# Layer-norm row work of an attention stage moved to other slots and engines: ScalarE in two passes with an fp32 intermediate, GpSimd for the low part, SyncE for loads and stores

## The chip, the cores and the metric

The kernel runs on one core of one Trainium2 chip. The metric is the device time of one execution in microseconds (us). The core's engines are PE (TensorE), DVE (VectorE), ACT (ScalarE), POOL (GpSimd) and SP (SyncE, which here issues DMAs and computes nothing). Each runs its own list of instructions in order; they meet through semaphores.

## The reference, cut to what matters

```python
def reference(x, txt, ...):
    h = _L0_tok_ref(log_dt, Lambda, x, 1024)            # a kernel of 1024 positions from 64 modes, 32 x 128 rows
    h = jnp.concatenate([h, txt], axis=1)                # 32 batches of 128 + 77 = 205 rows of 1024
    h = h + _L0_attn_ref(_layernorm(h), wq, wk, wv, wo)  # causal, 32 query heads of 32, 8 key heads
    h = h + _L0_ffn_ref(_layernorm(h), W_base, b_base, enc0, enc1, coefs0, coefs1, mask0, mask1)
    return h

def _layernorm(x, axis=-1, eps=1e-05):
    m = jnp.mean(x, axis=axis, keepdims=True)
    v = jnp.var(x, axis=axis, keepdims=True)
    return (x - m) / jnp.sqrt(v + eps)
```

Everything is fp32 in and out. The kernel multiplies in fp16 pairs: a value is split into a high part (rounded to fp16) and a low part (what is left, also fp16), and a product is three products, high*high, high*low and low*high.

## The kernel before

Three stages run one after the other, with a barrier between them. `ssm` (about the first 185 us) computes the first 128 rows of each batch and writes them to `hcat` in DRAM. `attention` (about 185 to 1740 us) works through the 32 batches and writes to `acat`. `tail` (the rest) does the output projection and the second residual block over 52 tiles of 128 rows. The change touches `attention` and a little of `ssm`.

`attention` is a software pipeline written out by hand. Step b (from -4 to 32) works on several batches at once, each with its part of the work, and `parts(b)` says which parts a step has:

- `att`: scores, exponentials and weighted values of batch b;
- `max`: score rows and their maxima of batch b+1 (a max per row is folded into the score product as two further rows of `qst`);
- `qkv`: query, key and value units of batch b+2 (8 query units, 2 key, 2 value; a unit is 24 matmuls of 205 columns into one of two PSUM banks `psJ`);
- `turn`: DMA transposes of the normalized rows of batch b+3, from `xfh`, `xfl` (high, low) to `xth`, `xtl`;
- `ln`: layer-norm statistics and the split of batch b+4;
- `load`: rows of batch b+5 from `hcat` into `xin` (two buffers).

A step has eight slots, g = 0 to 7, one per key head. In slot g every engine does its share for that head. PE (`step`, L1059 to L1106): two score products (`scores`, L981), maxima products (L1024 to L1031), first half of the slot's query unit, the third score product (L984), more maxima products, second half of the unit, the weighted values of the head before (`weigh`, L1010), then any second or third unit of the slot. ACT: three exponentials into `p32` (L783), three fp16 copies of the masked result into `ph` (L790), then an fp16 copy of each unit (L798). POOL: three causal masks (L699) and the low parts of the second and third block, `pl` (L704). DVE: the maxima (`take_maxes`, L879 and L885), the low part of the first block (L936), `norm` of the head before (L833, L836), and the low part of each unit (`split_unit`, L893), which waits for ACT's copy. The last unit of a slot is split late, in the next slot behind the first maxima. `EXTRA` puts the four value and key units into slots 0 to 3, as a second unit; the transposed maxima (unit kind "m") lie in slots 0 and 4.

The row work of layer norm in the kernel before:

- statistics on DVE in slots 1 to 3 (`layer_norm`, L841), the last of them the first guess of a reciprocal square root;
- `scale_rows` on POOL behind slot 3 (L669): twelve chained operations on 128x2 (`rsqrt_rounds`) and the negated mean;
- `high_part` on ACT (L723), one of four pieces (two row tiles by two halves of 512 columns) in each of slots 4 to 7: subtract the mean in place (L732), then multiply by the scale into fp16 `xfh` (L734);
- `low_part` on DVE (L858): multiply by the scale and subtract `xfh`, into `xfl` (L862). Piece 0 in slot 6, pieces 1 and 2 in slot 7, piece 3 in slot 0 of the next step;
- `turn` on SP (L632) near the start of the next step: four DMA transposes.

SP's list in a step, in order (L583 to L626): keys and queries of the second half restacked (L578), max rows of half 1 (L629, L630), at one step the loads of the tail's weights (`ahead`, L604), `turn` of both row tiles, keys and queries of the first half restacked, four transposes of the values (L622), max rows of half 0. ACT issues the loads of `xin` (L714, L715) in slot 3 and the stores of `ao` (L720, L721) in slots 2 and 6, and copies the values to `vh`, `vl` (`values`, L742) at the head of slot 2.

Before the first step ACT makes the high parts of the query weights (`weights_high(0)`), DVE their low parts (`weights_low(0)`), and the first rows are loaded, normalized, split and turned. In `ssm`, `weight_peak` (L370) takes the largest weight in the last 12 of 16 chunks, and SP sends the two peaks through DRAM (L174, L176) before the last chunk's stores.

## Time and profile before

| | |
|---|---|
| median of 3 runs | 2897.89 us (2894.68 to 2900.92) |
| the profiled execution | 2894.3 us, of which the span of instructions is 2891.9 us |
| mean granted clock of PE | 0.975 |
| busy over the span | PE 92%, PE weight load 66%, DVE 67%, ACT 43%, POOL 40% |

```profile
## 2 busy tenths in 40 slices
PE   1948999999999999999999976999999999999999
DVE  8966888888888888888888674644444444444443
ACT  4343676766767676766667572201000010101010
POOL 2751565656656565666656570101010101010100
PEclk9979999999999999999999976999999999999999
DMA  7756556465555555565555454454545455545553
```

A digit is the busy share of a slice of 72.3 us in tenths; PEclk is the granted clock in tenths. Slices 5 to 22 are the attention stage in its steady state. PE is over 90% busy there, DVE 80 to 90%. A matmul's duration in this profile is longer than its pitch (252 ns against 88 ns for 205 columns), so a wait of PE shows shorter than the time it costs; time lost is best read from start to start.

### The profile page before, as it was taken

To read this page: it belongs to the slowest core of one execution; us is meant where nothing else is said; L and a number is where in the kernel's file an instruction comes from. 1 tells how busy PE (TensorE), PEld (TensorE's weight loads), DVE (VectorE), ACT (ScalarE), POOL (GpSimd) and SP (SyncE) were. 2 spreads that over 40 slices of the span, in tenths; PEclk is the share of its full clock that TensorE was granted. 3 is DMA by queue.
4 is the path that set the end of the run, shared out by engine and by line. 5 is a ranking of instruction groups with operands and counts; after the bars stand their busy time and mean duration, and the time that the engine had idled before them with its cause. 6 is when DMAs were issued, how large, how long until landed. Compare 5 with 4: busy or idle time off the path is not lost. (4 is left out here: it accounts for less than half of the span.)

```text
span 2891.9 us, 70053 instructions
## 1 busy us (share of the span) xinstructions
PE 2655.3 (92%) x27456; PEld 1919.6 (66%) x27456; DVE 1941.2 (67%) x5569; ACT 1230.0 (43%) x2570; POOL 1144.9 (40%) x1810
## 2 busy tenths in 40 slices
PE   1948999999999999999999976999999999999999
PEld 1838888888888888888888952444444444444444
DVE  8966888888888888888888674644444444444443
ACT  4343676766767676766667572201000010101010
POOL 2751565656656565666656570101010101010100
PEclk9979999999999999999999976999999999999999
DMA  7756556465555555565555454454545455545553
GB/s 242 194 122 100 98 92 105 85 109 93 96 94 96 103 93 104 84 107 92 101 92 86 73 124 170 113 139 116 133 122 136 119 134 121 133 123 131 125 129 77
DMA packets 509031, 332.99 MB, mean 115 GB/s; under 512 B 421145, under 2 KB 464409, under 8 KB 508225
## 3 DMA queue, kind: packets, MB, share of 16 engines
q1 hardware_dynamic: 486192, 264.68, 46.3%
q10 hardware_dynamic: 22512, 63.84, 7.1%
q8 instruction: 219, 3.59, 0.6%
q14 instruction: 108, 0.88, 0.1%
HBM read 116.49 MB, written 80.61 MB: 68 GB/s over the span
## 5 line engine op out<-in xcount | busy, mean ns | idle before, releaser
L1044 PE MATMUL psJ<-xth,qh 128*128 128x205 f16 x2048 | 517.3, 253 | 51.6 <-DMA xtl<-xfl 47.6
L704 POOL TENSOR_TENSOR pl<-arena,ph 128x410 f16<-128x410 f32 (+1 forms) x512 | 501.0, 998 | 94.7 <-ACT ph L790 94.7
L1046 PE MATMUL psJ<-xth,ql 128*128 128x205 f16 x2048 | 516.3, 252 | 0.0
L1045 PE MATMUL psJ<-xtl,qh 128*128 128x205 f16 x2048 | 515.8, 252 | 0.0
L699 POOL TENSOR_SCALAR_AFFINE_SELECT arena<-arena 128x256 f32<-128x256 f32 (+1 forms) x768 | 331.7, 438 | 438.3 <-ACT arena L783 419.3
L1261 POOL TENSOR_TENSOR arena<-stage,arena 128x1024 f32<-128x1024 f32 x52 | 122.1, 2349 | 936.2 <-DVE stage L1304 936.2
L1275 ACT CAST xh<-arena 128x1024 f16<-128x1024 f32 x52 | 54.3, 1045 | 995.1 <-DVE arena L1313 995.1
L783 ACT ACTIVATE arena<-psT,escale 128x410 f32<-128x410 f32 (+1 forms) x768 | 399.6, 565 | 95.5 <-PE psT L984 57.5
L790 ACT CAST ph<-arena 128x410 f16<-128x410 f32 (+1 forms) x768 | 334.8, 500 | 14.9 <-POOL arena L699 14.7
L1304 DVE SCALAR_TENSOR_TENSOR stage<-ps5O,osc,h_in 128x512 f32<-128x512 f32 x104 | 77.9, 750 | 388.4 <-PE ps5O L1401 388.4
L885 DVE TENSOR_REDUCE mx<-psS 77x2 f32<-77x410 f32 x512 | 296.5, 579 | 60.7 <-PE psS L1031 57.0
L1399 PE MATMUL ps5F<-wfh,xth 128*128 128x512 f16 x832 | 315.4, 379 | 3.4 <-DMA xtl<-xl 2.3
L1400 PE MATMUL ps5O<-wol,ath 128*128 128x512 f16 x832 | 316.1, 380 | 0.0
L1399 PE MATMUL ps5O<-woh,ath 128*128 128x512 f16 x832 | 316.1, 380 | 0.0
L1401 PE MATMUL ps5O<-woh,atl 128*128 128x512 f16 x832 | 316.0, 380 | 0.0
L1400 PE MATMUL ps5F<-wfl,xth 128*128 128x512 f16 x832 | 315.3, 379 | 0.0
L1401 PE MATMUL ps5F<-wfh,xtl 128*128 128x512 f16 x832 | 315.3, 379 | 0.0
L879 DVE CUSTOM_DVE_ANT_0 seen<-psS,mask 128x128 bf16<-128x128 f32 x1024 | 235.4, 286 | 82.7 <-PE psS L1024 82.0
L1010 PE MATMUL psO<-vh,ph 128*128 128x33 f16 (+1 forms) x3072 | 261.0, 178 | 5.0 <-issue 4.6
L1010 PE MATMUL psO<-vl,ph 128*128 128x33 f16 (+1 forms) x3072 | 260.0, 178 | 0.0
L1010 PE MATMUL psO<-vh,pl 128*128 128x33 f16 (+1 forms) x3072 | 260.0, 178 | 0.0
L1046 PE MATMUL psJ<-xth,kl 128*128 128x205 f16 x1024 | 257.8, 252 | 0.0
(231 smaller groups left out, 6106.2 us busy)
## 6 DMA issues: line engine op xcount, KB each, us to landing
a_in<-acat SPq DMA_DIRECT2D x52, 512.0 KB, 3.8
h_in<-hcat SPq DMA_DIRECT2D x52, 512.0 KB, 4.6
qst<-qsh SPq DMA_DIRECT2D x128, 205.0 KB, 4.7
out<-stage SPq DMA_DIRECT2D x51, 512.0 KB, 3.1
hcat<-ob SPq DMA_DIRECT2D x64, 256.0 KB, 4.4
xin<-hcat ACTq DMA_DIRECT2D x32, 512.0 KB
acat<-arena ACTq DMA_DIRECT2D x64, 256.0 KB
qst<-qsl SPq DMA_DIRECT2D x64, 205.0 KB, 5.7
```

What stands on the lines that cost most here:

```text
L699: pool.affine_select(out=v, in_=v, compare_op=ALU.is_ge, fill=0.0, base=0, pattern=[[0, v.shape[1]], [1, w]], channel_multiplier=-1).then_ ...
L704: pool.tensor_tensor(view(pl, g % 2, k), view(p32, g % 2, k), view(ph, g % 2, k), ALU.subtract).then_inc(lo_pool, 1)
L783: act.activation(view(p32, g % 2, k), ps_view(psT[(g + k) % 2], k), ACT.Exp, scale=(escale[:, 0:1] if k < 2 else escale[0:TXT, 0:1])).then ...
L790: act.copy(view(ph, g % 2, k), view(p32, g % 2, k)).then_inc(hi_done, 1)
L885: dve.tensor_reduce(dst, v, AX.X, ALU.max).then_inc(s_read, 1)
L1010: m = pe.matmul(o[:, t, r, :], p, v[0:T[j], j, g, :], start=n == 0, stop=n == len(list_) - 1)
L1044: pe.matmul(ps[:, 0:S], wh[:, k, c], xth[:, par, k, 0:S], start=k == 0, stop=False)
L1045: pe.matmul(ps[:, 0:S], wh[:, k, c], xtl[:, par, k, 0:S], start=False, stop=False)
L1046: m = pe.matmul(ps[:, 0:S], wl[:, k, c], xth[:, par, k, 0:S], start=False, stop=k == KC - 1)
L1399: pe.matmul(ps[h][:], th[:, k, :], wh[:, k, c], start=k == 0, stop=False)
L1400: pe.matmul(ps[h][:], th[:, k, :], wl[:, k, c], start=False, stop=False)
L1401: m = pe.matmul(ps[h][:], tl[:, k, :], wh[:, k, c], start=False, stop=k == KC - 1)
```

## The change

- `high_part` now does both in fp32 first: one activation with scale and bias writes the normalized value in place, fp32, then a plain copy rounds it to `xfh`. For that `nmean` becomes minus mean times scale (one more small POOL operation per step), and `rs` and `nmean` get two buffers.
- The low part becomes a plain subtraction, `xin - xfh`. POOL does it (`low_rows`), except for the first batch, where DVE does (`low_part`).
- The row work is moved by a step: the pieces of `high_part` of batch b+3 run in slots 1, 2 and 3 (two pieces) of step b, behind the query unit's copy and ahead of the copy of the slot's second unit; the pieces of `low_rows` run at the ends of POOL's slots 2, 3 and 4 (two pieces), and `scale_rows` behind them in slot 4.
- The value and key units move from slots 0 to 3 into slots 1 to 4. In slots with several units DVE splits the query unit early, behind the low part of the first block.
- `values` is cut in two and moved behind the `ph` copies of slots 1 and 2.
- SP issues the loads of `xin` and the stores of `ao` instead of ACT. `turn` of the first row tile stays near the step's start, but each of its transposes waits for its own part; `turn` of the second tile goes behind the value transposes. The tail's loads go out one per step from step 1 on, and the largest (4 MB, output weights) at the end of step 29 instead of early in step 30.
- Start: DVE itself does the twelve chained operations for the first batch; half of the query weights' low parts are put behind the first row pieces; the first load is issued alone, the second when it has landed. In `ssm` the peaks are taken two chunks earlier and sent one chunk earlier.

```diff
-        EXTRA = {0: ("v", 0), 1: ("v", 1), 2: ("k", 0), 3: ("k", 1)}
+        EXTRA = {1: ("v", 0), 2: ("v", 1), 3: ("k", 0), 4: ("k", 1)}
+        HIGH, LOW, LINK = {1: (0,), 2: (1,), 3: (2, 3)}, {2: (0,), 3: (1,), 4: (2, 3)}, {1: 0, 2: 1, 3: 2}
+        FIRST_HIGH, FIRST_LOW = {2: (0,), 3: (1,), 4: (2, 3)}, {3: (0,), 4: (1,), 5: (2, 3)}
...
 # SP, step(b, par, has)
-                if b == B - 2:
-                    for q in v_in:
-                        sp.wait_ge(q, 32 * B)
-                    for dst, src, arrived in ahead:
-                        sp.dma_start(dst, src).then_inc(arrived, 16)
-                if has["turn"]:
+                if has["last"]:
+                    store(b - 1, 1)
+                if has["turn"] and b >= 0:
                     wait(sp, pj_filled, base)
                     turn(0, nxt, b + 3)
-                    turn(1, nxt, b + 3)
                 if has["qkv"]:
 ...                 # keys, queries of the first half restacked, as before
+                if has["turn"] and b < 0:
+                    wait(sp, pj_filled, base)
+                    turn(0, nxt, b + 3)
+                    turn(1, nxt, b + 3)
 ...                 # value transposes, as before
+                if has["turn"] and b >= 0:
+                    turn(1, nxt, b + 3)
                 if has["max"]:
                     wait(sp, pj_lo, base + at(rows, "m", 0) + 1)
                     shift_rows(0, nxt)
+                if has["att"]:
+                    store(b, 0)
+                if has["load"]:
+                    sp.wait_ge(x_lo, 4 * (b + 4))
+                    load(b + 5, 1 - par)
+                if 1 <= b < len(ahead):
+                    dst, src, arrived = ahead[b]
+                    sp.dma_start(dst, src).then_inc(arrived, 16)
...
             def turn(t, to, n):
+                sp.wait_ge(x_hi, 4 * n + 2 * t + 2)
+                sp.dma_start_transpose(out=xth[:, to, :, cols], in_=xfh[0:r, t, :]).then_inc(xt_in[t], 16)
                 sp.wait_ge(x_lo, 4 * n + 2 * t + 2)
-                sp.dma_start_transpose(out=xth[:, to, :, cols], in_=xfh[0:r, t, :]).then_inc(xt_in[t], 16)
                 sp.dma_start_transpose(out=xtl[:, to, :, cols], in_=xfl[0:r, t, :]).then_inc(xt_in[t], 16)
+            load(0, 0)
+            sp.wait_ge(x_in[0], 32)
+            load(1, 1)
...
 # POOL
+            def low_rows(m, n):
+                t, h = divmod(n, 2)
+                c, r = slice(h * D // 2, (h + 1) * D // 2), T[t]
+                pool.wait_ge(x_hi, 4 * m + n + 1)
+                pool.tensor_tensor(xfl[0:r, t, c], xin[0:r, m % 2, t, c], xfh[0:r, t, c], ALU.subtract).then_inc(x_lo, 1)
...
-                    if g == 3 and has["ln"]:
+                    if has["turn"]:
+                        for piece in LOW.get(g, ()):
+                            low_rows(b + 3, piece)
+                    if g == 4 and has["ln"]:
                         scale_rows(b)
...
 # ACT
-                act.activation(x, x, ACT.Identity, bias=nmean[0:r, t:t + 1]).then_inc(centred, 1)
-                act.wait_ge(centred, 4 * (b + 4) + n + 1)
-                act.activation(xfh[0:r, t, c], x, ACT.Copy, scale=rs[0:r, 3, t:t + 1]).then_inc(x_hi, 1)
+                act.activation(x, x, ACT.Identity, bias=nmean[0:r, m % 2, t:t + 1],
+                               scale=rs[0:r, m % 2, 3, t:t + 1]).then_inc(centred, 1)
+                act.wait_ge(centred, 4 * m + n + 1)
+                act.copy(xfh[0:r, t, c], x).then_inc(x_hi, 1)
...
-                    if g >= 4 and has["ln"]:
-                        high_part(b, par, g - 4)
+                        if i == 0:
+                            for piece in pieces:
+                                high_part(b + 3, piece)
...
 # DVE
+                    if b == -4:
+                        rsqrt_rounds(link, dve, rs[:, b % 2])
...
-                    if has["turn"] and g == 0:
-                        low_part(b + 3, 3)
+                    split = 0
+                    if len(rows[g]) > 1 and rows[g][0][0] == "q":
+                        split_unit(b, par, (k0 + n) % 2, *rows[g][0], base + n + 1)
+                        n += 1
+                        split = 1
-                        for piece in {6: (0,), 7: (1, 2)}.get(g, ()):
-                            low_part(b + 4, piece)
```

## Rows read from the trace of the kernel before

**Rows 1.** Waits of PE, 400 to 1600 us: total, times, longest
```profile
PE psS L1028 <- DVE mx L879: 37.0, 52, 1.1
PE psT L984 <- ACT arena L783: 28.9, 55, 1.1
```

**Rows 2.** PE in time through step 10: start, duration, line, shapes, [idle before]
```profile
750.11 0.33 PE L981 MATMUL psT<-qst,kst 98*128 98x410 f16 x1
...
753.37 0.23 PE L1028 MATMUL psS<-mask,ident_bf 77*77 77x154 bf16 x1 [1.08 <-DVE mx L879]
...
757.93 0.34 PE L981 MATMUL psT<-qst,kst 98*128 98x410 f16 x1
...
764.29 0.34 PE L981 MATMUL psT<-qst,kst 98*128 98x410 f16 x1
...
771.57 0.34 PE L981 MATMUL psT<-qst,kst 98*128 98x410 f16 x1
...
777.94 0.34 PE L981 MATMUL psT<-qst,kst 98*128 98x410 f16 x1
...
779.82 0.30 PE L984 MATMUL psT<-qst,kst 98*77 98x308 f16 x1
...
782.35 0.34 PE L981 MATMUL psT<-qst,kst 98*128 98x410 f16 x1
...
796.52 0.33 PE L981 MATMUL psT<-qst,kst 98*128 98x410 f16 x1
```

**Rows 3.** DVE groups by line, 400 to 1600 us: busy, mean ns, idle before
```profile
L862 DVE SCALAR_TENSOR_TENSOR xfl<-xin,rs,xfh 128x512 f16<-128x512 f32 (+1 forms) x104 | 126.4, 1235 | 0.0
```

**Rows 4.** ACT in time, slots 3 and 4 of the step
```profile
774.22 1.30 ACT L790 CAST ph<-arena 128x410 f16<-128x410 f32 x3
775.42 0.32 ACT L798 CAST qsh<-psJ 128x205 f16<-128x205 f32 x1
778.14 0.33 ACT L798 CAST ksh<-psJ 128x205 f16<-128x205 f32 x1 [2.39 <-PE psJ L1046]
...
781.07 1.32 ACT L790 CAST ph<-arena 128x410 f16<-128x410 f32 x3 [0.40 <-POOL arena L699]
...
782.78 0.70 ACT L732 ACTIVATE xin<-xin,nmean 128x512 f32<-128x512 f32 x1
```

**Rows 5.** POOL in time, slots 3 and 4 of the step, then slot 7
```profile
775.25 1.73 POOL L704 TENSOR_TENSOR pl<-arena,ph 128x410 f16<-128x410 f32 x2 [0.38 <-ACT ph L790]
777.09 0.19 POOL L1135 TENSOR_TENSOR rs<-rs 128x2 f32<-128x2 f32 x1
...
780.40 0.22 POOL L673 TENSOR_SCALAR nmean<-mv 128x2 f32<-128x2 f32 x1
...
795.47 3.11 POOL L704 TENSOR_TENSOR pl<-arena,ph 128x410 f16<-128x410 f32 x2 [0.38 <-ACT ph L790]
```

**Rows 6.** SP's DMA issues in time, slots 4 and 5 of the step
```profile
779.90 6.78 SPq L622 DMA_TRANSPOSE vt<-stage  x4
786.73 0.59 SPq L629 DMA_DIRECT2D qst<-mh  x1
```

**Rows 7.** DMA issues of the execution: count, size, median us to landing
```profile
qst<-ml SPq DMA_DIRECT2D x64, 6.4 KB, 1.9
```

**Rows 8.** Tile xtl: issue of its transposes on SP, ns min/median/max
```profile
L636 SPq DMA_TRANSPOSE xtl<-xfl x64: 1281/1448/3170, 212.6 to 1604.7; - x64
```

**Rows 9.** The start of the attention stage in time: DVE, POOL, SP, PE
```profile
192.26 1.42 DVE L852 BATCH_NORM_STATS2 stats<-xin 128x6 f32<-128x512 f32 x2 [4.39 <-DMA xin<-hcat]
...
196.31 1.29 POOL L1135 TENSOR_TENSOR rs<-rs 128x2 f32<-128x2 f32 x1 [1.18 <-DVE rs L1128]
...
215.26 1.34 SPq L636 DMA_TRANSPOSE xtl<-xfl  x1
...
223.92 0.33 PE L1044 MATMUL psJ<-xth,qh 128*128 128x205 f16 x1 [47.64 <-DMA xtl<-xfl]
```

**Rows 10.** PE in time: the start of step 31
```profile
1712.06 0.52 PE L981 MATMUL psT<-qst,kst 98*128 98x410 f16 x1 [4.09 <-DMA qst<-ml]
```

More of the change, by code:

```diff
@@ L616, in step @@
                     restack(Q_PARTS, qst[par][:, 0], HALVES[0], q_in[0])
+                if has["turn"] and b < 0:
+                    wait(sp, pj_filled, base)
+                    turn(0, nxt, b + 3)
+                    turn(1, nxt, b + 3)
+                if has["qkv"]:
+                    wait(sp, pj_lo, base + at(rows, "v", 1) + 1)
                     wait(sp, v_ok, 2 * (b + 2))
@@ L626, in step, with load, store @@
                     shift_rows(0, nxt)
+                if has["att"]:
[6 more added lines that the diff above has]
+                    sp.dma_start(dst, src).then_inc(arrived, 16)
+                if b == B - 3:
+                    for q in v_in:
+                        sp.wait_ge(q, 32 * B)
+                    dst, src, arrived = ahead[0]
+                    sp.dma_start(dst, src).then_inc(arrived, 16)
+            def load(b, par):
+                sp.dma_start(xin[:, par, 0, :], hcat[b * S:b * S + P, :]).then_inc(x_in[par], 16)
+                sp.dma_start(xin[0:TXT, par, 1, :], hcat[b * S + P:b * S + S, :]).then_inc(x_in[par], 16)
+            def store(b, half):
+                c = slice(half * D // 2, (half + 1) * D // 2)
+                sp.wait_ge(norm_done, 8 * b + 4 * half + 4)
+                sp.dma_start(acat[b * S:b * S + P, c], ao[:, half, 0, :]).then_inc(a_out[half], 16)
+                sp.dma_start(acat[b * S + P:b * S + S, c], ao[0:TXT, half, 1, :]).then_inc(a_out[half], 16)
             def shift_rows(half, to):
@@ L678, in step @@
                 if not has["att"]:
-                    if has["ln"]:
+                    if has["ln"] and b > -4:
                         scale_rows(b)
+                    if has["turn"] and b > -3:
+                        for piece in range(4):
+                            low_rows(b + 3, piece)
                     if b == -4:
-                        pool.memset(ph[:], 0.0)
-                        pool.memset(pl[:], 0.0)
+                        pool.memset(ph[:, :, 2, :], 0.0)
+                        pool.memset(pl[:, :, 2, :], 0.0)
                     if b == -3:
@@ L759, in step @@
                 if b == -3:
+                    for n in range(4):
+                        high_part(0, n)
+                    n = 0
                     weights_high(1)
@@ L765, in step @@
                 for g in SLOTS:
-                    if g == 3 and has["load"]:
-                        act.wait_ge(x_lo, 4 * (b + 4))
-                        load(b + 5, 1 - par)
-                    if g == 2 and has["last"]:
-                        store(b - 1, 1)
-                    if g == 2 and has["max"]:
-                        values(b + 1)
-                    if g == 6 and has["att"]:
-                        store(b, 0)
                     if has["att"]:
@@ L790, in step @@
                             act.copy(view(ph, g % 2, k), view(p32, g % 2, k)).then_inc(hi_done, 1)
-                    for kind, m in rows[g]:
+                    if g in (1, 2) and has["max"]:
+                        values(b + 1, g - 1)
+                    pieces = (HIGH if b >= 0 else FIRST_HIGH).get(g, ()) if has["turn"] and b > -3 else ()
+                    if not rows[g]:
+                        for piece in pieces:
+                            high_part(b + 3, piece)
+                    for i, (kind, m) in enumerate(rows[g]):
                         src, hi, _ = unit_views(kind, m, (k0 + n) % 2, b, par)
@@ L799, in step @@
                         n += 1
-                    if g >= 4 and has["ln"]:
-                        high_part(b, par, g - 4)
+                        if i == 0:
+                            for piece in pieces:
+                                high_part(b + 3, piece)
             steps(act, step)
@@ L814, in _, with weights_low @@
             dve.wait_ge(cleared, 1)
-            def weights_low(n):
-                for k in range(KC):
+            def weights_low(n, ks):
+                for k in ks:
                     dve.wait_ge(w_hi, n * KC + k + 1)
@@ L939, in step @@
                         take_maxes(b, j, base, (0, 1), late_read)
[L940 to L950 removed]
+                    split = 0
[3 more added lines that the diff above has]
+                        split = 1
+                    if b == -3 and g == 0:
+                        for part, ks in (((0, 1), (4, 5)), ((2, 3), (6, 7))):
+                            for piece in part:
+                                low_part(0, piece)
+                            weights_low(0, ks)
+                        weights_low(1, range(KC))
+                    if has["ln"] and g in LINK:
+                        layer_norm(b, par, LINK[g])
+                    if b == -4 and g == NKV - 1:
+                        weights_low(0, range(4))
                     if has["att"] and g:
```

66 lines of the change are left out of this document (28 added, 38 removed).

## The prediction

> **What bounds the kernel now.** I read the busy digits first: in the attention stage PE is above 90% in every slice at the full clock, DVE nearly so, and the tail behind it is PE alone. The change leaves the tail as it is, so only three places can move: the steady steps of attention, the stage's start, and its last steps. Next the waits of PE in the steady stage [rows 1]: there are two kinds only, PE waiting for DVE's maxima (52 times in 26 steps, two per step) and for ACT's exponentials (55). Together they show 65.9 us of idle, 2.5 us per step. Then PE in time through one step [rows 2], since durations hide part of a wait. The step takes 796.52 - 750.11 = 46.41 us. Slots 1 and 3 have no gap: 6.36 and 6.37 us with a second unit. Slot 4, without one but with the transposed maxima (about 0.18), takes 4.41, so a plain slot costs 4.23 and a second unit 2.13. A clean slot 0 would be 4.23 + 2.13 + 0.18 = 6.54; it took 7.82: 1.28 lost, with PE waiting for maxima at 753.37. Slot 2 took 7.28 instead of 6.36: 0.92 lost, waiting for exponentials. Slots 5 to 7 took 14.17 instead of 12.69: 1.48 lost. In all 3.7 us of 46.4 are gaps, and 42.7 is the floor that PE's own work sets.
>
> **Part 1, what the moves remove.** DVE's low parts are 4 per step at 1.235 us [rows 3], 4.9 us. They stand in slots 6, 7 and 0, just where DVE is late with its maxima, so with them the gap of slot 0 and most of slot 7's go: I take 1.7 us. The gap of slot 2 comes from ACT issuing two stores and copying values ahead of its exponentials; both are moved away: 0.9. The gaps of slots 5 and 6 come from ACT's row pieces ahead of the next exponentials, two passes of 0.70 [rows 4], 1.4 us each. In slots 1 to 3 there is an idle stretch of 2.39 us per slot, in which ACT waits for the second unit [rows 4]. A piece and half of `values` (about as long as a `ph` copy, 1.30 / 3) fit in it with 0.5 to spare; two pieces (2.8, less what a plain copy saves against a scaled one, unknown) in slot 3 run 0.4 over, which the exponentials' lead over PE covers. Gain 0.8. I leave 0.2 for waits of DVE on the later unit copy (values and the early split stand between). So 3.7 becomes 0.2 if nothing new is late.
>
> **Part 2, what is late instead: POOL in slot 4.** The subtraction of 512 columns costs POOL 1.2 us: its two `pl` subtractions (410 and 308 columns) take 1.73 together [rows 5], 2.4 ns per column. Four pieces add 4.8 us per step to an engine that is busy 5 to 6 tenths of these slices: as a sum it fits. But where they lie counts. In slot 3 (start 771.57) POOL ends its `pl` at 776.98, 5.4 us behind the slot's start, and `scale_rows` runs from 777.09 to 780.62, 3.5 us [rows 5]. After the change slot 4 has 5.4, then two pieces (2.35), then `scale_rows` with one more operation (3.8): it ends 11.65 us after the slot's start. Slot 4, now with a second unit, lasts 6.54. The masks of slot 5 are wanted 1.15 us into it, at 7.7, so they are 4.0 us late. The kernel before shows what lateness does: there `scale_rows` makes the masks of slot 4 about 1.5 late, and ACT's `ph` copy comes at 781.07, 3.13 behind the slot's start of 777.94, where slot 3 has it at 774.22, 2.65 behind its start [rows 2, 4]. So 1.0 of the lateness is free, 0.5 is passed on, and PE does not yet stall. With 4.0 it is 3.0 that is passed on. Queued behind the waiting copies are, on ACT, the unit's copy (it ends some 4.05 into a slot on time, 775.42 + 0.2 [rows 4]) and the exponentials of slot 6, and on DVE the low part of the first block, `norm` and the maxima of slot 6. PE wants the first exponential of slot 6 at 1.88 into it (779.82 - 777.94 [rows 2]) and the first maxima right behind that. ACT: the unit's copy ends at 3.0 + 4.05 = 7.05, the exponential takes 0.6, 7.65 against 4.23 + 1.88 = 6.11: 1.55 late. DVE: its low part follows the first `ph` copy, at 3.0 + 3.2, and low part, `norm` and first maxima take some 2.0 (the sum of their means), 8.2 against 6.25: 1.95 late. I take a stall of 2.0 per step. Bounds: if a piece costs 1.0 and the chain 3.5, the stall is 1.3; beside DVE's low part the same two subtractions needed 3.11 [rows 5], 4.3 ns per column, and if that pace held for the pieces (2.2 each), it is 4.0.
>
> The Trainium skill speaks against this move: "GPSIMD Engine Reference", section 4.1 (Engine selection), gives elementwise work with two inputs to VectorE and calls GpSimd about 2 times slower. The rows here do not show that for these two operations, since DVE's piece has a mean of 1235 ns [rows 3] against my 1.2 us on POOL. By the rule a piece would take some 2.5 us, an estimate from the page's factor, and the time would be that of rival B's far end and some 10 more. Another rule speaks for it: "SBUF — State Buffer", section "Who interferes with whom", says that a DVE instruction with two SBUF inputs and a GpSimd instruction that reads SBUF exclude each other. By it the pair at 795.47 was held by DVE's low part, and relief comes with the move.
>
> **Part 3, SP's list.** It gets six more issues per step and two of four row transposes behind the values. Counted from slot 4's start: keys of the first half go at 2.5 (the key unit is one slot later), three issues of 0.6, queries follow to 6.4; the value transposes take 6.78 [rows 6] to 13.2; the second tile's two transposes about 3.4 (median 1.448, up to 3.170 [rows 8]) to 16.6; the max rows twice 0.6 to 17.8, landing 1.9 after the second's issue [rows 7], at 19.1. PE wants them at the head of the next step, 6.54 + 3 x 4.23 = 19.2 without a stall, 21.2 with the stall of part 2. Before, the first max row was issued at 786.73 [rows 6], 8.8 behind slot 4's start. So nothing is lost here, but the slack of some 10 us is gone. Loads and stores behind it have until the next step's slot 1 and later: cost nothing. `xt` of the second tile lands at about 18.5, also in time.
>
> **Sum, steady.** Per step 3.7 becomes 2.2: a gain of 1.5. Row work exists in steps 0 to 28, 29 steps: 43 us.
>
> **Part 4, the start.** PE waits 47.64 us, until 223.92 [rows 9]. The peaks' round trip held the last stores: 1.2 earlier. The statistics start at 192.26, after 4.39 of waiting for the first load, with both loads in flight [rows 9]; alone it lands perhaps 2 earlier (bounds 0 and 3). The twelve links on POOL took from 196.31 to 207.4, 11.1 us for what takes 3.5 in a steady step, beside DVE's weight parts [rows 9]; on DVE, at about 0.2 per link, 2.6. So ACT starts its pieces at about 195.7 and ends at 201. DVE then does 4 weight parts (4.8), pieces and the other four (6.8) until about 208; the last row transpose goes at about 206 instead of 215.26 and lands at 210. PE starts 14 earlier. Part is given back: in the steps below 0, SP puts four transposes (5.3) between the queries and the values, so the max rows of step -1 leave that much later and PE waits about 3.5 for them at step 0, and some 2 for the rows at step -1. I keep 9 (4 to 14).
>
> **Part 5, the end.** The 4.09 us at the head of step 31 is PE waiting for max rows that stood behind the tail's loads [rows 10]; these are elsewhere now. The 4 MB load at the end of step 29 puts the restacked keys behind it, wanted 17 us later: 1 us lost perhaps. Net 3 (-3 to 4).
>
> Total 43 + 9 + 3 = 55. Against the profiled execution's 2894.3 us that is 2839.3; the median of three is 3.6 above it, which I carry along: 2843.
>
> **Rivals.**
> - A, POOL's overrun does not bind (pieces or chain are shorter, or the lead is larger than I read): the gaps fall to 0.2 to 0.8. For: POOL is busy 5 to 6 tenths of the time. Against: the 0.40 that ACT already waits for masks in slot 4 [rows 4]. At 0.3: 3.4 x 29 = 99, with 12: 2787.
> - B, POOL's pieces cost nearly twice what I take, because DVE's subtraction or its small operations hold POOL or run into it: stall 3.0 to 4.0. For: 3.11 against 1.73 for the same pair [rows 5]. Against: that pair ran beside DVE's low parts, which are gone. At 3.6 the gaps are 3.8, and only start and end are left: 3 lost, 12 gained, 2889.
> - C, slower, by SP: the transposes issued back to back go at the pace of the slowest, not of the mean. Six at 2.7 instead of 1.7 make the max rows land at 6.4 + 16.2 + 0.6 + 1.9 = 25.1, against 21.2: PE stalls 3.9 in every slot 0, 6.1 of gaps against 3.7, +70 less 12: 2956. It loses from about 2.5 per transpose on. Against: four take 6.78 [rows 6], 1.7 each.
>
> **How the numbers follow.** My case 0.57 (its own range 2815 to 2875: stall of 1.3 to 3.0, start 5 either way); A 0.18 (2775 to 2815); B 0.15 (2875 to 2905); C 0.10. The range for 8 in 10 is 2785 to 2893: below it about a third of A, above it C and the slower half of B. What can be told from no change is 0.2%, 5.8 us. Faster: my case, A and the nearer 0.09 of B, 0.84; same 0.05, of B; slower 0.11, nearly all C.
>
> **What would show it.** Right: the low part of rows on POOL at about 1.2 us, PE's waits for maxima in slot 0 gone, one wait of about 2 us in slot 6, with ACT waiting for POOL's masks about 3 us in slot 5; a step of 45 us; PE's first attention matmul near 210. No wait in slot 6 and steps of 43 would be A; PE waiting at a step's head for `qst` or `xtl` would be C. Wrong would be a new gap in slots 1 to 3, where I count none.

## The result and the profile after

| | before | after |
|---|---|---|
| median | 2897.4 us (2894.7 to 2900.9, 4 runs) | 2846.1 us (2843.8 to 2847.4, 4 runs) |
| ratio after to before | | 0.982, 95% interval 0.980 to 0.984 |
| span of the profiled execution | 2891.9 us | 2844.2 us |
| mean granted clock of PE | 0.975 | 0.974 |
| first matmul of the stage | 223.9 us [rows 9] | 209.2 us |
| start of step 0 | 286.8 | 290.5 |
| mean step, from step 4's start to step 24's | 46.55 | 44.70 |
| start of step 29 | 1634.0 | 1586.4 |
| start of step 31 | 1712.1 | 1661.1 |

The change is 1.8% faster, 2846 us where 2843 was forecast. By stretches of the span, before less after: to step 0 -3.7, steps 0 to 28 51.3, steps 29 and 30 3.4, from step 31 on -3.3, in sum 47.7. The last term is no effect of the change that I can name: over all the kernels below that stretch takes 1179 to 1183.5 us, 1179.8 before and 1183.1 after.

The busy digits of the page, after (slices of 71.1 us):

```profile
DVE  8974677777777777777777765644444444444443
...
POOL 2742576766767667676676660100101010110100
```

In the attention stage DVE falls from 8 to 7 tenths and POOL rises from 5 or 6 to 6 or 7. PE's waits after, 400 to 1600 us (us in total, times, longest us), where [rows 1] had 37.0 and 28.9:

```profile
PE psT L1039 <- ACT arena L817: 28.0, 26, 1.1
PE psS L1083 <- DVE mx L927: 7.6, 26, 0.3
```

One pair of waits per step is left, and both stand at one place, slot 6. PE in time in the step from 649.76 to 694.39, after:

```profile
673.39 0.51 PE L1036 MATMUL psT<-qst,kst 98*128 98x410 f16 x2
...
679.94 0.51 PE L1036 MATMUL psT<-qst,kst 98*128 98x410 f16 x2
...
684.18 0.51 PE L1036 MATMUL psT<-qst,kst 98*128 98x410 f16 x2
...
687.32 0.33 PE L1039 MATMUL psT<-qst,kst 98*77 98x308 f16 x1 [1.09 <-ACT arena L817]
...
687.94 0.23 PE L1083 MATMUL psS<-mask,ident_bf 77*77 77x154 bf16 x1 [0.29 <-DVE mx L927]
...
690.16 0.51 PE L1036 MATMUL psT<-qst,kst 98*128 98x410 f16 x2
```

Slot 4 is 679.94 - 673.39 = 6.55, slot 5 4.24: no gap. Slot 6 takes 690.16 - 684.18 = 5.98 where 4.24 is clean, as steps 28 and 29 show, in which POOL has no chain: 1.74 lost. Behind it stands POOL, without a pause from slot 4's `pl` to the masks of slot 5, and ACT waiting for these:

```profile
677.06 1.69 POOL L753 TENSOR_TENSOR pl<-arena,ph 128x410 f16<-128x410 f32 x2 [0.38 <-ACT ph L824]
678.71 2.27 POOL L719 TENSOR_TENSOR xfl<-xin,xfh 77x512 f16<-77x512 f32 x2
...
684.58 0.20 POOL L713 TENSOR_TENSOR nmean<-nmean,rs 128x2 f32<-128x2 f32 x1
684.73 1.23 POOL L748 TENSOR_SCALAR_AFFINE_SELECT arena<-arena 128x256 f32<-128x256 f32 x3
```

```profile
685.23 1.32 ACT L824 CAST ph<-arena 128x410 f16<-128x410 f32 x3 [2.55 <-POOL arena L748]
```

The start of the stage is the other place. PE's waits after, 205 to 300 us, and its granted clock in stretches (PEclk is the column after POOL's):

```profile
PE psT L1036 <- DMA qst<-ml: 6.5, 1, 6.5
PE psS L1083 <- DVE mx L927: 3.7, 1, 3.7
```

```profile
255.00:260.00 5.00, 2.53 (x16) 2.28 (x17) 3.58 (x14) 0.00 (x0) 0.00 (x0) 0.67 0.47 74
260.00:265.00 5.00, 5.00 (x41) 4.58 (x39) 2.48 (x9) 1.99 (x4) 0.00 (x0) 0.65 0.00 0
```

These are means of each stretch. Taken from where PE goes on working, the granted clock stands at 0.50, the level of 1.2 GHz, until 263.5:

```profile
257.50:263.50 6.00, 6.00 (x36) 5.30 (x37) 3.05 (x7) 1.66 (x3) 0.00 (x0) 0.50 0.01 3
```

PE starts 14.7 earlier and is 3.7 late at step 0: 18.4 are given back. The trace accounts for nearly all of it. Between its first matmul and step 0 PE waits 17.1 us in all, 10.2 of them in the two waits above, and 3.1 in the kernel before: 14.0 more. And it works at the clock of 0.50 for 12.5 us (209.2 to 212.3, 219.2 to 222.6, 257.5 to 263.5), where before it was 4.3 (223.9 to 228.2); half of the difference, 4.1, is lost by that. Both long waits go back to SP's issues below step 0, the load of the next rows (L654) and the max rows (L664), which stand behind the value transposes:

```profile
243.20 5.04 SPq L631 DMA_TRANSPOSE vt<-stage  x4
248.28 0.59 SPq L654 DMA_DIRECT2D xin<-hcat  x1
...
287.86 0.60 SPq L664 DMA_DIRECT2D qst<-mh  x1
```

### The profile page after: what moved, and what is told of

Its sections match the earlier page's. It is cut to its first block and busy times, and to the rows that moved or that the text cites. A ratio compares the mean times of both kernels' runs of the same rounds, so it can differ in the third digit from the quotient of the medians.

```text
span 2844.2 us, 70178 instructions
## 1 busy us (share of the span) xinstructions
PE 2648.3 (93%) x27456; PEld 1926.5 (68%) x27456; DVE 1816.9 (64%) x5458; ACT 1231.1 (43%) x2570; POOL 1212.3 (43%) x1952
## 5 line engine op out<-in xcount | busy, mean ns | idle before, releaser
L817 ACT ACTIVATE arena<-psT,escale 128x410 f32<-128x410 f32 (+1 forms) x768 | 407.8, 568 | 183.4 <-PE psT L1039 146.1
L753 POOL TENSOR_TENSOR pl<-arena,ph 128x410 f16<-128x410 f32 (+1 forms) x512 | 437.3, 874 | 92.6 <-ACT ph L824 92.6
L1099 PE MATMUL psJ<-xth,kh 128*128 128x205 f16 x1024 | 258.9, 253 | 2.0 <-DVE qsl L941 2.0
```

The source lines that it names most:

```text
L753: pool.tensor_tensor(view(pl, g % 2, k), view(p32, g % 2, k), view(ph, g % 2, k), ALU.subtract).then_inc(lo_pool, 1)
L817: act.activation(view(p32, g % 2, k), ps_view(psT[(g + k) % 2], k), ACT.Exp, scale=(escale[:, 0:1] if k < 2 else escale[0:TXT, 0:1])).then ...
L1099: pe.matmul(ps[:, 0:S], wh[:, k, c], xth[:, par, k, 0:S], start=k == 0, stop=False)
```

## The experiments

In the table "lost in slots" is the mean time per step (steps 2 to 29, both included) by which PE's starts in a slot stand further apart than the same pair of instructions does where nothing is waited for; only slots that lose 0.1 or more are named, 0.1 in slot 0 left out. A wait at the head of slot 0 counts to slot 0. Mean step is as above. Ratios are to the kernel before, with 95% intervals.

| kernel | ratio | step 0 | mean step | lost in slots |
|---|---|---|---|---|
| before | 1 | 286.8 | 46.55 | 0: 1.21; 2: 0.97; 5: 0.53; 6: 0.32; 7: 0.46 |
| after | 0.982 (0.980 to 0.984) | 290.5 | 44.70 | 6: 1.60 |
| x1_split | 0.968 (0.966 to 0.970) | 289.6 | 43.35 | 0: 0.24; 1: 0.17; 2: 0.13 |
| x2_slot6 | 0.986 (0.985 to 0.988) | 292.7 | 45.25 | 0: 2.08; 1: 0.15 |
| x3_dve_low | 0.973 (0.971 to 0.974) | 289.4 | 43.81 | 3: 0.52; 6: 0.26 |
| x4_start | 0.977 (0.976 to 0.979) | 283.1 | 44.75 | 6: 1.57 |
| x5_both | 0.964 (0.962 to 0.965) | 281.8 | 43.22 | 0: 0.18; 1: 0.22 |
| x6_form | 1.000 (0.999 to 1.001) | 289.5 | 46.55 | 0: 1.27; 2: 0.95; 5: 0.75; 6: 0.45 |
| x7_moves | 0.986 (0.984 to 0.987) | 289.3 | 45.11 | 0: 1.21; 5: 0.53; 7: 0.46 |
| x8_form_pool | 0.987 (0.985 to 0.989) | 289.2 | 45.24 | 2: 0.92; 5: 0.75; 6: 0.44 |
| x9_early | 0.983 (0.981 to 0.985) | 281.2 | 44.86 | 0: 1.56; 2: 0.40 |
| x10_dve_split | 0.969 (0.968 to 0.971) | 280.4 | 43.84 | 0: 0.18; 1: 0.25; 3: 0.49 |

### Is it POOL's queue in slot 4? Rounds apart

```diff
-                    if g == 4 and has["ln"]:
-                        scale_rows(b)
+                    if g >= 5 and has["ln"]:
+                        if g == 5:
+                            pool.wait_ge(dve_ln, 9 * (b + 5))
+                        scale_round(b, g - 5)      # one of three rounds; nmean with the last
```

> The changed kernel with POOL's scale_rows taken apart: its three rounds run in slots 5, 6 and 7, one in each (the two nmean operations with the last), in place of all fourteen operations in slot 4. Theory P (POOL's overrun in slot 4 is the cause of the 1.60 us gap that the changed kernel shows in slot 6): each slot now gets 1.1 us at most behind its low parts, the gap of slot 6 goes, a step takes 43.0 in place of 44.6, and 29 steps give 46 us: 2800 us. Rival Q (the gap comes from POOL and DVE or ACT holding each other while the low rows are subtracted, not from the length of the queue): nothing moves, 2846. Rival S (SP's list is at its limit, its max rows land 19.1 us behind slot 4's start where PE then wants them at 19.2): a part comes back as a wait for qst at the step's head, up to 1 us per step, 2800 to 2830.

2808.7 us against 2902.9 of before in the same comparison, ratio 0.968. PE's waits in the same stretch, 400 to 1600 us:

```profile
PE psS L1090 <- DVE mx L934: 3.2, 4, 1.8
PE psT L1043 <- DMA qst<-ml: 2.3, 3, 1.0
```

The 28.0 and 7.6 are gone, with the same operations on the same engine. Theory P holds in its cause, Q falls. The gain is 37 us where P had 46: the three waits for `qst` are rival S in small, whose range of 2800 to 2830 holds the result. SP's rows now come just in time or up to 1.0 late.

### The whole chain in another slot

```diff
-                    if g == 4 and has["ln"]:
+                    if g == 6 and has["ln"]:
                         scale_rows(b)
```

> The changed kernel with scale_rows as a whole moved from slot 4 to slot 6. Theory P: the low rows alone end 5.4 + 2.3 = 7.7 us behind slot 4's start, just when slot 5's masks are wanted, so slot 6's gap goes; but fourteen operations in one plain slot end 5.4 + 3.8 = 9.2 behind slot 6's start, where slot 7's masks are wanted at 5.4, 3.8 late, nearly as late as now (4.0). So the gap only moves two slots on, to slot 0: step 44.4, 2840 to 2846 us. Rival Q2 (only the sum of low rows and rounds in the one slot binds, either alone is within the lead): no gap anywhere, step 43.0, 2800.

2860.2 us, ratio 0.986: theory P, and Q2 falls. POOL's masks, wanted in slot 7, begin only at 698.94. ACT behind them, then PE in the next slot 0:

```profile
699.44 1.32 ACT L824 CAST ph<-arena 128x410 f16<-128x410 f32 x3 [2.60 <-POOL arena L748]
```

```profile
701.54 0.33 PE L1039 MATMUL psT<-qst,kst 98*77 98x308 f16 x1 [0.77 <-ACT arena L817]
```

The picture of slot 6, two slots on: fourteen dependent small operations, 3.8 us of POOL at 0.27 each, cost about the same behind a long slot with low rows as behind a plain one without. It came out 0.4% slower than after, where I had expected none to 0.2% faster: slot 0 loses 2.08 rather than 1.6, and step 0 began 2.2 later. There is one effect more that no theory had. From 294.3 to 1642.5 us the kernel after runs at the full clock, in spite of its waits of about 1 us. Here the granted clock fell to 0.50 seven times in the steady stage, six times behind the waits at slot 0 and once behind one for `qst`. One of these stretches is 1019.8 to 1023.2. The six steps of the first kind take 46.1, where most others take 44.9. That is some 7 of the 14 us by which this kernel is slower than after.

### Low parts on DVE

```diff
 # POOL, steps with attention
-                    if has["turn"]:
-                        for piece in LOW.get(g, ()):
-                            low_rows(b + 3, piece)
 # DVE, behind norm
+                    if has["att"] and has["turn"]:
+                        for piece in LOW.get(g, ()):
+                            dve.wait_ge(x_lo, 4 * (b + 3))
+                            low_part(b + 3, piece)
```

> The changed kernel with the low part of the rows subtracted by DVE in the steps of attention (the plain subtraction, in the same slots 2, 3 and 4, behind norm), and POOL keeping only scale_rows there. Theory P: POOL ends slot 4 at 5.4 + 3.8 = 9.2 where 7.7 is wanted, 1.5 late, about as in the kernel before, where that passed without a gap; the gap of slot 6 falls from 1.60 to 0 to 0.4, and DVE has room for four subtractions of about 0.7 in the long slots: step 43.0 to 43.4, 2800 to 2812 us. Rival D (DVE is what needed the relief, so GpSimd's part is what the change lives on): DVE is late with its maxima in slots 3 to 5, the step is 44.6 or longer, 2846 or more.

2821.5 us, ratio 0.973: 9 us above P's range, 0.9% faster than the change as made, and far from D. Slot 6 keeps 0.26, inside the 0 to 0.4 of P; slot 3 loses 0.52 for DVE's maxima, which I had not counted. The subtraction on DVE (ns min/median/max) and on POOL in the kernel after (group by line: busy, mean ns):

```profile
L908 DVE TENSOR_TENSOR xfl<-xin,xfh x120: 675/681/920, 202.5 to 1546.7; 128x512 f16<-128x512 f32 x60, 77x512 f16<-77x512 f32 x60
```

```profile
L719 POOL TENSOR_TENSOR xfl<-xin,xfh 128x512 f16<-128x512 f32 (+1 forms) x107 | 122.7, 1157 | 0.0
```

### The start

```diff
 # SP, b < 0: order of the issues
+                if has["max"] and b < 0:
+                    wait(sp, pj_lo, base + at(rows, "m", 0) + 1)
+                    shift_rows(0, nxt)
+                if has["load"] and b < 0:
+                    sp.wait_ge(x_lo, 4 * (b + 4))
+                    load(b + 5, 1 - par)
                 if has["qkv"]:
                     wait(sp, pj_lo, base + at(rows, "v", 1) + 1)
 ...
-                if has["max"]:
+                if has["max"] and b >= 0:
 ...
-                if has["load"]:
+                if has["load"] and b >= 0:
```

> The changed kernel with SP's order changed below step 0 only: the max rows of the first half and the next load of rows go right behind the row transposes, ahead of the value transposes. Theory T (what PE gained by starting 14.7 earlier was given back to SP's order: 3.7 us at 257 for a load issued at 248.28, 6.5 us at 290 for rows issued at 287.86, and the clock lowered after these waits): both waits fall under 1.5 us, step 0 starts 9 to 12 us earlier, 2834 to 2837 us. Rival U (these waits only stand in for later ones, because the value copies of step 0 or the row transposes are next): 0 to 3 us faster, 2843 to 2846.

2835.1 us, ratio 0.977 against 0.982; step 0 starts 7.4 earlier than after. PE's waits from 200 to 300 us, and the two stretches whose clock had fallen:

```profile
PE psT L1043 <- DMA qst<-ml: 1.2, 1, 1.2
```

```profile
255.00:260.00 5.00, 5.00 (x60) 4.88 (x58) 4.07 (x15) 1.14 (x5) 0.00 (x0) 1.00 0.83 125
260.00:265.00 5.00, 5.00 (x60) 4.87 (x59) 4.06 (x15) 1.94 (x5) 0.00 (x0) 1.00 0.07 9
```

6.5 became 1.2, 3.7 is gone, and the clock is whole where it was 0.67 and 0.65; it is at 0.50 from 248.8 to 252.2 instead. Theory T, with 7.4 where I had written 9 to 12. Even so the edit brings more than 7.4: PE's first matmul came at 211.8 here and at 209.2 in after, in a part that the edit leaves alone (it lies between 209.2 and 211.8 in all kernels with the changed start). From the first matmul to step 0 it is 71.3 us against 81.3. In the same way it is 79.0 to 81.7 in x1_split, x2_slot6 and x3_dve_low, without this edit, and 70.6 to 71.5 in x5_both, x9_early and x10_dve_split, with it.

### Both together

The edits of x1_split and x4_start.

> The two edits together: scale_rows taken apart over slots 5 to 7, and SP's order changed below step 0. Theory (two separate losses): the gains add up, 1.41% from the first and 0.49% from the second, ratio to the kernel before 0.963, about 2791 us. Rival S (with a shorter step SP's list is the next limit, and waits for qst at the step's head take the place of the gain): 0.966 or more, 2799 or more.

2794.2 us, ratio 0.9637 (0.9623 to 0.9652): the two gains add up (0.982 less 0.014 less 0.005 is 0.963). This is the best kernel of the study, 3.6% under before and 1.9% under the change. It has nothing left in reserve at SP: in a step whose successor starts at 1189.88 the last max row is issued at 1187.49 (SP's issues) and lands 2.3 later, at 1189.83. PE's waits for such rows, 400 to 1600 us:

```profile
PE psT L1050 <- DMA qst<-ml: 5.0, 2, 4.3
```

### The form alone

```diff
 # kernel before; ACT, DVE, POOL
-                act.activation(x, x, ACT.Identity, bias=nmean[0:r, t:t + 1]).then_inc(centred, 1)
+                act.activation(x, x, ACT.Identity, bias=nmean[0:r, t:t + 1],
+                               scale=rs[0:r, 3, t:t + 1]).then_inc(centred, 1)
-                act.activation(xfh[0:r, t, c], x, ACT.Copy, scale=rs[0:r, 3, t:t + 1]).then_inc(x_hi, 1)
+                act.copy(xfh[0:r, t, c], x).then_inc(x_hi, 1)
-                dve.scalar_tensor_tensor(xfl[...], xin[...], rs[...], xfh[...], ALU.mult, ALU.subtract)
+                dve.tensor_tensor(xfl[...], xin[...], xfh[...], ALU.subtract)
-                pool.tensor_scalar(nmean[:], mv[:, :, 0], -1.0, None, ALU.mult).then_inc(ln_done, 1)
+                links(pool.tensor_scalar(nmean[:], mv[:, :, 0], -1.0, None, ALU.mult))
+                pool.tensor_tensor(nmean[:], nmean[:], rs[:, 3], ALU.mult).then_inc(ln_done, 1)
```

> The kernel before with the form alone: ScalarE writes the normalized fp32 rows and copies them to fp16, nmean is multiplied by rs on POOL, and DVE's low part is the plain subtraction in its old place (slots 6, 7 and 0 of the next step). The plain subtraction took DVE 0.724 in the run with low parts on DVE, against 1.235 before: 4 x 0.51 = 2.0 us of DVE per step less where it is late. Theory F: the gap of slot 0 and a part of slot 7's shrink by 1.0 to 1.5 of the 3.7 us per step, 2855 to 2868. Rival N (the gaps there come from the order of the waits, not from the length of the subtraction): 2890 to 2897.

2898.1 us, ratio 1.000 (0.999 to 1.001). Theory F falls, and so does N's reason, since slot 7 did gain: 0.46 to 0.05. The mean of DVE's subtraction fell only from 1235 [rows 3] to 1048 ns, not to 0.724. DVE and POOL in the same stretch, slots 7 and 0:

```profile
752.21 2.06 DVE L864 TENSOR_TENSOR xfl<-xin,xfh 128x512 f16<-128x512 f32 x2
...
757.75 1.25 DVE L864 TENSOR_TENSOR xfl<-xin,xfh 77x512 f16<-77x512 f32 x1
```

```profile
752.19 2.71 POOL L705 TENSOR_TENSOR pl<-arena,ph 128x410 f16<-128x410 f32 x2 [0.38 <-ACT ph L792]
...
756.42 2.04 POOL L705 TENSOR_TENSOR pl<-arena,ph 128x410 f16<-128x410 f32 x2 [0.35 <-ACT ph L792]
```

In the old places the subtraction runs beside POOL's `pl` pair in slots 7 and 0. In slot 0 it still takes 1.25, nearly as long as the scaled form, and slot 0 keeps its gap (1.27). What slot 7 gained, slots 5 and 6 lost (0.53 to 0.75, 0.32 to 0.45): ACT's waits for POOL's masks rose from 11.3 to 17.7 us in 26 steps, 0.25 per step, about what the chain's one further operation takes (0.3). That the second follows from the first is worked out, not tried.

### GpSimd's subtraction in the old places

```diff
 # the kernel of x6_form; POOL, steps with attention
+                    if g == 0 and has["turn"]:
+                        low_rows(b + 3, 3)
                     if g == 3 and has["ln"]:
                         scale_rows(b)
+                    if g > 4 and has["ln"]:
+                        low_rows(b + 4, g - 5)
 ...                 # low_rows as in the change; the steps below 0 likewise
 # DVE: its low_part calls go, and its statistics wait for the row pieces of ACT
+                        wait(dve, x_hi, 4 * (b + 4))
```

> The kernel before with the form and GpSimd's subtraction, in the old places: low parts on POOL behind the pl subtractions of slots 5, 6, 7 and of slot 0 of the next step, ACT's row pieces, values, stores and loads where they were. Theory: the gap of slot 0 and slot 7's, 1.7 us per step together, go; slot 2's 0.9 and the 0.8 of ACT's row pieces in slots 5 and 6 stay; POOL is up to 1.2 late per slot, within or just over its lead: step 44.7 to 45.2, 2848 to 2863. Rival D (POOL, with one piece in each of three plain slots, adds up its lateness there and ACT's exponentials wait): 2863 to 2890.

2861.8 us, ratio 0.987. As the theory has it: slots 0 and 7 from 1.67 together to 0.01, the others as in x6_form. PE's waits, 400 to 1600 us, for ACT now (0.2 for another):

```profile
PE psT L996 <- ACT arena L799: 38.6, 80, 1.2
```

Three pieces in three plain slots, 1.2 each, did not add up.

### The moves of values, stores and loads alone

```diff
 # kernel before; ACT
-                    if g == 3 and has["load"]:
-                        act.wait_ge(x_lo, 4 * (b + 4))
-                        load(b + 5, 1 - par)
-                    if g == 2 and has["last"]:
-                        store(b - 1, 1)
-                    if g == 2 and has["max"]:
-                        values(b + 1)
-                    if g == 6 and has["att"]:
-                        store(b, 0)
 ...
+                    if g in (1, 2) and has["max"]:      # behind the ph copies
+                        values(b + 1, g - 1)
 # SP issues the loads and stores, as in the change
```

> The kernel before with one move alone: value copies behind the ph copies of slots 1 and 2, one in each, and loads and stores issued by SP; rows, their low parts and units where they were. Theory: ACT is no longer late with the exponentials of slot 2, its 0.92 us go: 0.9 x 31 = 28, 2870. Rival M (DVE's low parts make everything late anyway, and the time comes back as a wait for maxima in slots 2 or 3): 2885 to 2897.

2858.7 us, ratio 0.986, where I had expected 2870: slot 2's 0.97 went, and slot 6's 0.32 with it. ACT had a store to issue at the head of slot 6 too, which is all that this edit takes out of slot 6, and the row pieces, which are still in slots 4 to 7 here, were not to blame for it. PE's waits, 400 to 1600 us:

```profile
PE psS L1027 <- DVE mx L878: 36.9, 52, 1.1
```

### Max rows earlier

```diff
 # the kernel of x5_both; SP, b >= 0
+                    if has["max"] and b >= 0:
+                        wait(sp, pj_lo, base + at(rows, "m", 0) + 1)
+                        shift_rows(0, nxt)
                     for c in range(2):
                         for k in range(2):
                             sp.dma_start_transpose(...)     # values
```

> The kernel with both edits and one more: in steps with attention SP issues the max rows of the first half ahead of the four value transposes, in place of behind them and the second tile's row transposes. Theory S (SP's list is the next limit: the last max row is issued 2.4 us before the step's head and lands about 1.9 later, and in two steps of the steady stage PE waited 5.0 in all for it): these waits go, steps are 43.1 without exceptions, 3 to 6 us faster, 2788 to 2791. Rival V (values and second row tile, now 1.3 later, are missed instead, by ACT's value copies or PE's first unit): 2794 or more, with a wait for xtl or v_ok in slots 0 to 2.

2845.9 us, ratio 0.983: 52 us slower than x5_both. Rival V, which had 2794 or more. SP's issues, PE's first row-fed matmul, and PE's waits for this line from 400 to 1600 us:

```profile
1205.09 0.58 SPq L674 DMA_DIRECT2D qst<-mh  x1
...
1213.89 1.28 SPq L680 DMA_TRANSPOSE xth<-xfh  x1
```

```profile
1218.07 0.25 PE L1116 MATMUL psJ<-xth,qh 128*128 128x205 f16 x1 [1.86 <-issue]
```

```profile
PE psJ L1116 <- issue: 31.6, 23, 2.5
```

SP was ready for the max rows at 1202.54, the end of its last issue for the queries, but their low part came only at about 1205.1: 2.5 us in which its list stood still. With the rows' own 1.6, the second tile's last transpose is issued at 1215.22, where the next step starts at 1215.23, and lands at 1217.98; PE, which waits for it, goes on at 1218.07. The profile puts this wait to "issue"; that it is the transpose is read from these times. In five steps of the stage the granted clock then fell to 0.50 for a few us, and these take 46.3 to 46.8. The 0.40 that slot 2 loses was not followed up. What was mended (5 us in the whole stretch) was far smaller than what the new order cost.

### What GpSimd's part is worth once the rounds are apart

The kernel of x5_both with the edit of x3_dve_low.

> The kernel with both edits, but the low part of the rows on DVE in the steps of attention (slots 2 to 4, behind norm) in place of POOL: what GpSimd's subtraction is worth once the rounds are spread. Theory: with the rounds spread nothing of POOL binds either way; DVE's two pieces make it late by the 0.52 that slot 3 showed with low parts on DVE, all else as in the kernel with both edits: step 43.4 to 43.6, 8 to 15 us slower than that, 2802 to 2809. Rival E (the sum of DVE's work has room, 0.52 came from the rounds in POOL's slot 4): within 3 us of it, 2792 to 2797.

2809.0 us, ratio 0.969 against 0.964. As the theory has it, at the edge of its range: 0.49 in slot 3, slot 6's 0.26 gone.

PE's waits for maxima from 400 to 1600 us are 11.8 us in 27 cases, its waits for `qst` 1.2 in two.

## Why the prediction was right, and where it was not

**The total.** 2846 against 2843, in the likeliest case (steady 43, start 9, end 3). That it is so near is luck in part: the steady steps brought 51.3 where 43 stood, and the start lost 3.7 where 9 were to be gained. The end's 3.4 against 3 is as forecast, and 3.3 are scatter of the tail. So the span gained 47.7 where the sum had 55, and about half of what is missing was covered by the 3.6 that I had carried along from the median before.

**Part 1.** The 1.7 for DVE's low parts is confirmed alone: between x6_form and x8_form_pool slot 0 gives back 1.26, and from before to x8_form_pool slots 0 and 7 give back 1.66. The 0.9 of slot 2 is confirmed by x7_moves, 0.97. The 0.8 put to ACT's row pieces in slots 5 and 6 was right as a sum (0.85) and wrong in its cause by 0.32: slot 6 lost that to the store issued at its head (x7_moves). I had read only slot 2 for stores. Taking the moves one by one, before loses 3.5 per step in the table's mean; low parts to POOL take 1.66 off, values and stores 1.29. The rest, 0.53 in slot 5, I put to the move of the row pieces; no run moves them alone. What is left of the old gaps in the kernel after is about 0.2, as forecast.

**Part 2.** The mechanism holds in each of its links, and x1_split and x2_slot6 show that it is the whole of the gap: without the queue in slot 4 nothing is left, and moved to slot 6 it returns at slot 0. POOL's end behind slot 4's start is 684.58 + 0.20 - 673.39 = 11.4: the two pieces start at 5.3 and take 2.27, the chain 3.8. The forecast has 11.65 for it, though its own terms, 5.4, 2.35 and 3.8, add up to 11.55. ACT's copy stands at 685.23 - 679.94 = 5.29 behind slot 5's start, 2.64 later than the 2.65 of a slot on time [rows 4], where I had 3.0. Of these 0.36 less 0.26 show at PE, 1.74 lost in a step with the chain in place of 2.0. The chain stands in steps 0 to 27, one fewer than the 29 I counted, since step 28 has no statistics to finish (its slot 6 takes 4.24); the table's 1.60 is the mean with steps 28 and 29. In all 28 x 1.74 = 48.7 us are lost where 29 x 2.0 = 58 stood, and these 9 less account for the 8 us between 43 and 51.3.

The price of the piece was right (1.157 for 1.2), the comparison with DVE was not. I set POOL's 1.2 against DVE's 1235 ns and concluded that GpSimd was as fast. DVE's plain subtraction takes 0.681 as a median and 0.724 as a mean (x3_dve_low). The 1235 was the scaled form beside POOL's own subtractions, and it is mostly the neighbour that made it long, not the form: at the start of the stage, where POOL subtracts nothing, the scaled form took 0.75 in the kernel before, and the plain one 0.69 in x6_form. Before, DVE:

```profile
209.00 0.75 DVE L862 SCALAR_TENSOR_TENSOR xfl<-xin,rs,xfh 128x512 f16<-128x512 f32 x1 [3.09 <-ACT xfh L734]
```

I had put POOL's 3.11 down to its neighbour, and not DVE's own mean. The Trainium skill's factor of about 2 ("GPSIMD Engine Reference", section 4.1) is, for this operation, 1.6 to 1.7 in these runs (1.157 against 0.724 and 0.681). So as built, GpSimd's subtraction costs more than it saves: it adds 2.3 to the slot that already has the chain, and x3_dve_low, without it, is 0.9% faster. Once the chain is spread it is worth 0.6% (x5_both against x10_dve_split). It paid also in the old places, 1.3% (x8_form_pool against x6_form).

**Part 3.** SP's list holds, by the margin that was worked out: the last max row was issued at 689.62, 16.2 behind slot 4's start, and landed at 692.50, 19.1 behind it, the forecast's own number, 1.9 before the step starts at 694.39. Two errors meet in that: the issue came earlier than the 17.2 of the working, and the landing took 2.9 (2.7 as a median of the execution), not the 1.9 of [rows 7]. After, issue to landing:

```profile
qst<-ml SPq DMA_DIRECT2D x64, 6.4 KB, 2.7
```

1.7 of the margin is given by the stall. So without the stall next to nothing is left, and single steps in x1_split and x5_both wait for `qst`. Rival C did not come in the changed kernel, but x9_early shows what it would do: some 4 us more in front of the second tile cost 1.6 per step and 52 us in all.

**Part 4 failed.** PE began at 209.19, 14.7 earlier, as written (14), and link by link: the peaks 1.2 earlier, the statistics at 189.43 in place of 192.26, the first row piece on ACT at 196.75 (195.7 forecast), the last row transpose issued at 206.26 (206) and landed at 208.95 (210). The step that failed is the give-back: 5 forecast, 18.4 measured. I had the 3.5 for max rows at step 0 (6.5 measured) and 2 for rows at step -1 (2.9, behind the transposes, landed at 244.65), but missed two things. The load of the next rows is the last entry of SP's list in each of these short steps, and DVE, whose statistics stand ahead of its maxima, waited 3.80 for it:

```profile
254.70 1.42 DVE L896 BATCH_NORM_STATS2 stats<-xin 128x6 f32<-128x512 f32 x2 [3.80 <-DMA xin<-hcat]
```

And behind PE's wait of 3.69 the granted clock was at 0.50, the level of 1.2 GHz, until 263.5; in x4_start, without the wait, it was 1.00 there. x4_start takes 9.0 us of these waits away, and from the first matmul to step 0 it recovers 10.0 of the 18.4, so they did not stand in for others, as rival U had it. What is left, 8.5, no run takes away. By the trace of x4_start, 5.3 of it are waits (8.4 in all before step 0, against 3.1 in the kernel before, most of them for row transposes and for DVE's low parts), and 2.7 the clock of 0.50, at which PE works 9.7 us in place of 4.3.

**Part 5.** The 4.09 of [rows 10] went, and a new wait came half a step earlier, where I had 1 for the restacked keys behind the 4 MB load. SP and PE, after:

```profile
1625.44 0.41 SPq L651 DMA_DIRECT2D stage<-in_L_attn_wo  x1
...
1635.86 0.72 SPq L665 DMA_DIRECT2D qst<-ml  x1
```

```profile
1645.01 0.86 PE L1036 MATMUL psT<-qst,kst 98*128 98x410 f16 x2 [2.78 <-DMA qst<-ml]
```

A transfer of 6.4 KB issued at 1635.86 came 9.1 us later, at 1644.96; the load of 4 MB, issued ahead of it at 1625.44, landed at 1642.64. It was the max rows, not the keys; with the value work of steps 29 and 30 also off ACT's slot 2 (step 29 went from 43.99 to 42.87) the net is 3.4.

**The rivals.** A: POOL's queue does bind, but what A asked for is had by spreading it, 2809 (x1_split). B: POOL's pieces ran at 1.157 and not at twice that, since DVE's low parts were no longer beside them. C: above.

## What to carry to other kernels

- An engine with idle time in sum can still set the pace by one queue in one slot. Ask of each added piece when the next thing that others wait for is due on that engine, and spread a chain of small dependent operations over several slots: here the same operations in three slots in place of one gave 1.4%.
- Separate form, engine and place before crediting one of them. The form alone gave nothing, engine 1.3% in one place and a loss in another, and the plainest move (issues and copies off the engine that produces for PE) 1.4%.
- What an earlier start is worth is read at the first steady step. Follow each queue entry of the ramp up to there, the next loads too, before booking it.

## What the runs showed of the hardware that I had not expected

- DVE's subtraction of 512 columns with two SBUF inputs took 0.681 us as a median in x3_dve_low and 1.25 beside POOL's `pl` pair (x6_form, slot 0). The pair took 2.04 and 2.71 there, against 1.69 in the kernel after. The Trainium skill has this as mutual exclusion ("SBUF — State Buffer", section "Who interferes with whom"); the durations agree.
- A small operation with one input can be held as well. DVE's second guess operation, on two columns, takes 168 ns at the least, and 1.8 us in the steps after, where it took 0.8 before. After, POOL's low rows follow the `pl` at once, and it ends with them (DVE and POOL in time, after):

```profile
671.73 1.81 DVE L1182 TENSOR_SCALAR rs<-rs 128x2 int32<-128x2 int32 x1
```

```profile
672.36 1.16 POOL L719 TENSOR_TENSOR xfl<-xin,xfh 128x512 f16<-128x512 f32 x1
```

671.73 + 1.81 = 673.54, and 672.36 + 1.16 = 673.52. It cost nothing here: slots 3 and 4 of this step take 6.36 and 6.55, without a gap.
- A wait of PE of 3.69 us was followed by 6.0 us of work at a granted clock of 0.50: 3.0 us more, on top of the wait. Waits of about 1 us, one or two in each step, left the clock at 1.00 all through the steady stage in the kernels before and after, and in x2_slot6, with waits up to 1.6, it fell seven times. What decides between them these runs do not show.
